# Graph attention with masks from an adjacency matrix: the pair of heads that GpSimd masks is scored and released first, and the second A pair stands between the two mask groups of the other pair

## The reference

```python
qkv = layer_norm(x, g1, be1) @ w_qkv
q, k, v = ...                                   # n x 8 x 16 each
scores = einsum('nhd,mhd->hnm', q, k) * SCALE
scores = where(adj != 0, scores, -inf)
attn = softmax(scores, axis=-1)
out = einsum('hnm,mhd->nhd', attn, v).reshape(n, 128)
x = x + out @ w_proj + b_proj
x = x + gelu(layer_norm(x, g2, be2) @ w1 + b1) @ w2 + b2
```

## Time and profile before

| what | value |
|---|---|
| median of 3 runs | 3741.22 us (3737.74 to 3742.95) |
| profiled execution | 3741.04 us |
| its span, first to last instruction | 3739.3 us |
| mean granted TensorE clock | 0.944 |
| PE busy | 3467.5 us (93%) |
| DVE busy | 2969.6 us (79%) |
| POOL busy | 2489.5 us (67%) |
| ACT busy | 2334.8 us (62%) |

### The profile page before, as it was taken

One profiled execution on the slowest core, in us unless ns is written; L12 is line 12 of the kernel. 1 busy time (PEld: TensorE's weight loads), 2 busy tenths in 40 slices (PEclk: granted clock), 3 DMA queues, 4 the chain that ended last, 5 costly groups with the idle time before them and its releaser, 6 DMA issues.

```text
span 3739.3 us, 68583 instructions
## 1 busy us (share of the span) xinstructions
PE 3467.5 (93%) x22572; PEld 1404.7 (38%) x22572; DVE 2969.6 (79%) x8997; ACT 2334.8 (62%) x2596; POOL 2489.5 (67%) x1476
## 2 busy tenths in 40 slices
PE   6999999999999999997678999999999999999976
PEld 3443333333333333333434433333333333333234
DVE  6889898888888898841368999999999999999323
ACT  5358686868687777764241466666666666666732
POOL 1067877787878787885010578887878888878930
PEclk9589999999999999998896799999999999999988
DMA  4578787878787878662132546464646565545421
GB/s 137 169 238 259 244 260 236 257 232 263 222 278 221 278 224 281 215 195 76 57 104 87 176 136 190 140 192 139 187 142 183 146 187 147 180 148 175 117 65 51
DMA packets 480351, 676.31 MB, mean 181 GB/s; under 512 B 51552, under 2 KB 272864, under 8 KB 475616
## 3 DMA queue, kind: packets, MB, share of 16 engines
q1 hardware_dynamic: 479568, 671.83, 58.1%
q10 hardware_dynamic: 432, 0.10, 0.0%
HBM read 508.14 MB, written 165.68 MB: 180 GB/s over the span
## 4 chain that ended last, share of the span: by engine, by line
PE 39%; POOL 35%; issue 15%; DVE 7%; DMA 2%; POOLq 1%; ACT 1%; DVEq 0%; SPq 0%; ACTq 0%
POOL arena L921 35%; PE PS L464 12%; PE PS L444 9%; PE PS L477 7%; PE PS L471 6%; DVE spill L798 5%; PE PS L417 3%; POOLq L899 1%; PE PS L450 1%; DVE arena L758 0%; DVE neg_hi L806 0%; DMA arena<-out_dram 0%; PE PS L408 0%; ACT o_sb L673 0%; DMA mask<-in_adj_t 0%
## 5 line engine op out<-in xcount | busy, mean ns | idle before, releaser
L798 DVE CUSTOM_DVE_ANT_0 spill<-PS,mask_n 128x512 bf16<-128x512 f32 x4096 | 2635.8, 688 | 282.2 <-PE PS L444 182.3
L921 POOL TENSOR_TENSOR arena<-arena,mask 128x1024 int32<-128x1024 int32 x896 | 2137.8, 2386 | 646.4 <-ACT arena L665 641.3
L665 ACT ACTIVATE arena<-PS 128x1024 f32<-128x1024 f32 x2048 | 1991.3, 1022 | 919.0 <-PE PS L477 876.4
L444 PE MATMUL PS<-k_t,q_t 48*128 48x512 f32 x4096 | 1287.7, 546 | 61.7 <-DVE pmax L798 41.5
L464 PE MATMUL PS<-arena,v_sb 128*32 128x512 f32 x8192 | 1105.0, 612 | 41.7 <-ACT o_sb L673 37.6
L444 PEld LDWEIGHTS PS<-k_t,q_t 48*128 48x128 f32 x4096 | 546.4, 194 | 1028.8 <-DVE pmax L798 910.9
L471 PE MATMUL PS<-q_t,k_t 50*128 50x512 f32 x4096 | 931.6, 464 | 0.5 <-POOL arena L911 0.4
L477 PE MATMUL PS<-arena,idb 64*128 64x512 bf16 x4312 | 840.9, 390 | 0.0
L471 PEld LDWEIGHTS PS<-q_t,k_t 50*128 50x128 f32 x4096 | 400.2, 188 | 201.9 <-ACT arena L665 123.9
L477 PEld LDWEIGHTS PS<-arena,idb 64*128 64x128 bf16 x4312 | 209.0, 95 | 462.8 <-issue 337.9
L798 DVE DVE_READ_ACCUMULATOR2_ANT pmax<- 128x1 f32 x4096 | 340.1, 83 | 0.0
(11 more groups left out here) (54 smaller groups left out, 970.7 us busy)
## 6 DMA issues: line engine op xcount, KB each, us to landing
mask<-m_dram SPq DMA_DIRECT2D x768, 256.0 KB, 2.7
mask_n<-mn_dram SPq DMA_DIRECT2D x768, 128.0 KB, 2.7
adj_in<-in_adj SPq DMA_DIRECT2D x256, 256.0 KB, 3.8
mask<-in_adj_t SPq DMA_DIRECT2D x256, 256.0 KB, 4.0
m_dram<-mask SPq DMA_DIRECT2D x256, 256.0 KB, 3.7
mn_dram<-mask_n SPq DMA_DIRECT2D x256, 128.0 KB, 3.8
mt_dram<-arena SPq DMA_DIRECT2D x256, 128.0 KB, 3.5
arena<-mt_dram SPq DMA_DIRECT2D x256, 128.0 KB, 2.8
```

The lines of the kernel that those rows point to most:

```text
L444: pe.matmul(bank, q_t[r0:r0 + KROWS, gb % Q_SLOTS, pair, q * P:(q + 1) * P], k_t[r0:r0 + KROWS, pair, mb * TILE:(mb + 1) * TILE], start=Tr ...
L665: nc.scalar.activation(p_buf[:, t % P_SLOTS, 2 * half:2 * half + 2, :], ps_b[:, 2 * half:2 * half + 2, :], ACT.Exp, scale=SCALE).then_inc( ...
L798: dve.tensor_tensor_reduce(spill[:, j % A_BANKS, :], ps_a[:, j % A_BANKS, :], mask_n[:, v % N_SLOTS, :], 1.0, LOWEST, ALU.subtract, ALU.ma ...
L921: pool.tensor_tensor(p, p, m, ALU.mult).then_inc(p_masked, 1)
```

## The change

In every step the scores of heads 2 and 3 come first and the scores of heads 0 and 1 after them. In a pooled step heads 2 and 3 are released (`b_scored`) by their score matmul alone. The masks of heads 0 and 1 come last, and the second A pair now stands between their two groups. In an unpooled step the two groups for heads 2 and 3 also lie apart, with the scores of heads 0 and 1 between them. ACT takes the pairs in the new order, `mask_pair` waits for the first exponential of a step instead of both, and the wait for the mask tile (`t_made`, `mt_loaded`) stands behind the first scores.

```diff
--- before.py
+++ after.py
@@ -484,48 +484,45 @@
                 jobs = range(jobs_before(t), jobs_before(t + 1))
                 for j in jobs[:2]:
                     a_job(L, j)
+                if t > 0:
+                    pe.wait_ge(b_exped, L * 2 * STEPS + 2 * t - 1)
+                if s == 0:
+                    pe.wait_ge(a_done, L * NJ + JOB_AT["turn", nb, 2 * quad + 1] + 1)
+                score_b(L, t, 2)
+                mm = score_b(L, t, 3)
                 if L == 0:
                     pe.wait_ge(t_made, nb * MT + s + 1)
                 else:
                     pe.wait_ge(mt_loaded[s % 4], (nb * MT + s) // 4 * 16 + 16)
+                full = len(jobs) < 4
+                if pooled(L, t):
+                    mm.then_inc(b_scored, 1)
+                elif full:
+                    for j in range(2, 4):
+                        mm = pe.matmul(ps_b[:, j, :], idb[:], mask_t[:, s, :], start=False, stop=True)
+                    mm.then_inc(b_scored, 1)
+                else:
+                    add_mask(s, 2, 0), add_mask(s, 3, 1).then_inc(half_added, 1)
+                    added[0] += 1
                 if t > 0:
-                    pe.wait_ge(b_exped, L * 2 * STEPS + 2 * t - 1)
-                if s == 0:
-                    pe.wait_ge(a_done, L * NJ + JOB_AT["turn", nb, 2 * quad + 1] + 1)
+                    pe.wait_ge(b_exped, L * 2 * STEPS + 2 * t)
                 score_b(L, t, 0), score_b(L, t, 1)
-                if len(jobs) >= 4:
-                    add_mask(s, 0, 0), add_mask(s, 1, 1).then_inc(half_added, 1)
-                    added[0] += 1
-                    if t > 0:
-                        pe.wait_ge(b_exped, L * 2 * STEPS + 2 * t)
-                    score_b(L, t, 2), score_b(L, t, 3)
-                    pe.wait_ge(half_added, added[0])
-                    if pooled(L, t):
-                        add_mask(s, 1, 0), add_mask(s, 0, 1).then_inc(b_scored, 2)
-                        for j in jobs[2:]:
-                            a_job(L, j)
-                    else:
-                        add_mask(s, 1, 0), add_mask(s, 0, 1).then_inc(b_scored, 1)
-                        add_mask(s, 2, 0), add_mask(s, 3, 1).then_inc(half_added, 1)
-                        added[0] += 1
-                        for j in jobs[2:]:
-                            a_job(L, j)
-                        pe.wait_ge(half_added, added[0])
-                        add_mask(s, 3, 0), add_mask(s, 2, 1).then_inc(b_scored, 1)
-                else:
+                if full:
+                    for j in jobs[2:]:
+                        a_job(L, j)
                     for j in range(2):
                         mm = pe.matmul(ps_b[:, j, :], idb[:], mask_t[:, s, :], start=False, stop=True)
                     mm.then_inc(b_scored, 1)
+                else:
+                    if not pooled(L, t):
+                        pe.wait_ge(half_added, added[0])
+                        add_mask(s, 3, 0), add_mask(s, 2, 1).then_inc(b_scored, 1)
+                    add_mask(s, 0, 0), add_mask(s, 1, 1).then_inc(half_added, 1)
+                    added[0] += 1
                     for j in jobs[2:]:
                         a_job(L, j)
-                    if t > 0:
-                        pe.wait_ge(b_exped, L * 2 * STEPS + 2 * t)
-                    score_b(L, t, 2)
-                    mm = score_b(L, t, 3)
-                    if not pooled(L, t):
-                        for j in range(2, 4):
-                            mm = pe.matmul(ps_b[:, j, :], idb[:], mask_t[:, s, :], start=False, stop=True)
-                    mm.then_inc(b_scored, 1)
+                    pe.wait_ge(half_added, added[0])
+                    add_mask(s, 1, 0), add_mask(s, 0, 1).then_inc(b_scored, 1)
                 if t >= LAG:
                     gather_v(L, t - LAG)
 
@@ -658,9 +655,9 @@
                     keep_v(gi, g)
 
             def exp_pair(L, t, half):
-                k = L * 2 * STEPS + 2 * t + half
-                act.wait_ge(b_scored, k + 1)
-                if half == 0 and t >= P_SLOTS:
+
+                act.wait_ge(b_scored, L * 2 * STEPS + 2 * t + 2 - half)
+                if half == 1 and t >= P_SLOTS:
                     act.wait_ge(pv_done, L * STEPS + t - P_SLOTS + 1)
                 nc.scalar.activation(p_buf[:, t % P_SLOTS, 2 * half:2 * half + 2, :], ps_b[:, 2 * half:2 * half + 2, :],
                                      ACT.Exp, scale=SCALE).then_inc(b_exped, 1)
@@ -689,10 +686,10 @@
                     mask_rows(visits[made])
                     made += 1
                 for t in range(STEPS):
-                    exp_pair(L, t, 0)
+                    exp_pair(L, t, 1)
                     if t > LAG and t % MT == LAG:
                         keep_o(L, t // MT - 1)
-                    exp_pair(L, t, 1)
+                    exp_pair(L, t, 0)
                     while made < len(visits) and visit_step(visits[made]) - 3 < t + 1:
                         mask_rows(visits[made])
                         made += 1
@@ -911,7 +908,7 @@
                 pool.tensor_scalar(mask_t[:, s, :], m, -MASKED, MASKED, ALU.mult, ALU.add).then_inc(t_made, 1)
 
             def mask_pair(L, t):
-                pool.wait_ge(b_exped, L * 2 * STEPS + 2 * t + 2)
+                pool.wait_ge(b_exped, L * 2 * STEPS + 2 * t + 1)
                 if made(L, t):
                     pool.wait_ge(mask01_made, MADE[t + 1])
                 else:
```

## The result

| | before | changed |
|---|---|---|
| median | 3739.48 us | 3938.36 us (3935.46 to 3941.2, 4 runs) |
| span of the profiled execution | 3739.3 us | 3933.6 us |
| mean granted clock | 0.944 | 0.935 |

The ratio is 1.0531, 95% interval 1.0513 to 1.0549: 5.3% slower, 199 us. The sign was forecast, the size wasn't: 136 us were forecast, and the range ended at 3915.

What follows compares the result with a forecast made beforehand. Bound: an ACT-PE loop (2.76 us per pooled step), next the A-bank loop (2.71); crossed masks queued behind the fourth A score make 2.94. Terms +91, +41, +29, −6, −15, −4 sum to +136 us: 3877 us, range 3835 to 3915.

## What to carry to other kernels

Before moving work behind an instruction that waits, ask what filled that wait before: an engine that idles in the waiting loop doesn't make the loop shorter, and whatever is queued behind the waiting instruction is added to it. Follow the rare steps one by one as well as the regular ones: a tiny operation with a long duration can be a wait in disguise, and its length can change when another engine's phase moves. And here it paid to rewrite copying and two-operand VectorE work, where another engine waits for it beside a long GpSimd instruction, as one-operand reductions: 1% in the kernel before and 3% in the changed one.

## What I had not expected of the hardware

- A VectorE conversion of 128x16 numbers took 1.98 us beside GpSimd's multiplication and 0.17 without it, and ended 0.03 us after it; a two-operand maximum did the same, a reduction never.
- In two versions with the same waits and the same regular step, 92 us more at a granted clock of 0.50 cost 38 us.
- At 26 of 28 turns of the changed kernel with waits of 2.15 to 2.6 us the granted clock fell to 0.50, for 3.4 or 6.8 us; in the kernel before (waits of 0.96 to 1.72 us) at 14 of 27, for 3.4 us; with the waits gone, at none but the last turns.
- Two whole masks over all rows and the passage back to half-row matmuls took 0.54 us (2702.52 to 2703.06), against 0.50 for two crossed groups with the bare wait between (2701.40 to 2701.90).
